# A decoder's third stage: squaring and applying a triangular matrix in one product, without GpSimd's additions

## The reference, cut to what matters

```
def step(S, t):                      # one token of a chunk, all heads
    k_t, v_t, a_t, b_t = t
    S = S * a_t[:, :, None]
    kTS = jnp.einsum('bd,bde->be', k_t, S)
    S = S + (b_t * k_t)[:, :, None] * (v_t - kTS)[:, None, :]
```

## Time and profile before

| | us |
|---|---|
| three runs | 2650.59, 2654.94, 2660.51 |
| median | 2654.94 |
| span of the profiled execution | 2659.3 |
| third stage in it | 933.5 to 2659.3 |
| busy in the span: PE, DVE, ACT, POOL | 2338.5, 1532.4, 1679.5, 295.0 |

### The profile page before, as it was taken

How to read it: one execution, slowest core, us unless ns; L and a number is a source line. 1 busy time by engine, 2 the same in 40 slices (tenths; PEclk the granted TensorE clock), 3 DMA queues, 4 the chain that set the end, 5 groups by cost and what they waited for, 6 DMA issues and landing times.

```text
span 2659.3 us, 93159 instructions
## 1 busy us (share of the span) xinstructions
PE 2338.5 (88%) x41310; PEld 1738.7 (65%) x41314; DVE 1532.4 (58%) x3564; ACT 1679.5 (63%) x4172; POOL 295.0 (11%) x396
## 2 busy tenths in 40 slices
PE   3888889888888479999989999999999999999997
PEld 2666666666666257767767667777676676676775
DVE  3565656656565546555555665556656656655563
ACT  2778778777877245655656656556656566565563
POOL 0101010110100000110011001101110110011010
PEclk8999999999999689999999999999999999999997
DMA  3000000000000100000000000000000000000000
GB/s 111 8 9 9 8 9 9 10 8 9 9 8 7 50 7 9 7 7 7 6 9 7 7 9 7 7 6 6 9 8 6 9 7 7 9 7 7 6 6 4
DMA packets 55339, 29.77 MB, mean 11 GB/s; under 512 B 24224, under 2 KB 53216, under 8 KB 54944
## 3 DMA queue, kind: packets, MB, share of 16 engines
q1 hardware_dynamic: 50624, 21.90, 3.0%
q10 hardware_dynamic: 4320, 1.97, 0.3%
HBM read 18.60 MB, written 5.24 MB: 9 GB/s over the span
## 4 chain that ended last, share of the span: by engine, by line
PE 38%; DVE 13%; ACT 11%; issue 2%; DMA 0%; SPq 0%; DVEq 0%
PE bank L1130 5%; PE bank L1197 2%; PE bank L1327 2%; ACT PT L1382 2%; DVE h L1530 2%; DVE zels L462 2%; PE bank L358 2%; PE bank L1260 2%; ACT zels L1382 2%; DVE m L458 2%; PE bank L1246 1%; DVE h L1643 1%; PE bank L1320 1%; PE bank L1170 1%; PE bank L1229 1%
## 5 line engine op out<-in xcount | busy, mean ns | idle before, releaser
L1040 POOL TENSOR_TENSOR PT<-zels,unit 128x512 f32<-128x512 f32 x160 | 203.7, 1273 | 1472.3 <-ACT zels L1382 1284.1
L358 PE MATMUL bank<-w_gate,ident 128*128 128x256 f32 (+3 forms) x960 | 314.5, 411 | 0.0
L458 DVE TENSOR_REDUCE m<-bank 128x4 f32<-128x512 f32 x384 | 251.6, 683 | 39.7 <-PE bank L383 19.2
L393 PE MATMUL bank<-ident,zels 128*128 128x128 f32 x1536 | 226.3, 282 | 34.3 <-ACT zels L429 26.9
L1382 ACT ACTIVATE zels<-bank 128x512 f32<-128x512 f32 (+1 forms) x256 | 142.6, 573 | 158.8 <-PE bank L1246 82.6
L393 PEld LDWEIGHTS bank<-ident,zels 128*128 128x128 f32 x1536 | 168.3, 142 | 83.4 <-ACT zels L429 38.4
L437 ACT ACTIVATE PT<-bank 128x512 f32<-128x512 f32 x384 | 206.1, 629 | 3.8 <-PE bank L393 2.9
L1382 ACT ACTIVATE PT<-bank 128x512 f32<-128x512 f32 x256 | 147.8, 598 | 89.7 <-PE bank L1303 47.7
L433 ACT ACTIVATE zels<-zels 128x512 f32<-128x512 f32 x256 | 162.7, 646 | 55.5 <-DVE zels L462 55.1
L429 ACT ACTIVATE zels<-bank,m 128x128 f32<-128x128 f32 x512 | 148.0, 389 | 64.7 <-DVE m L458 64.7
L462 DVE TENSOR_TENSOR zels<-bank,m 128x512 f32<-128x512 f32 x256 | 177.0, 692 | 8.9
(11 more groups left out here) (293 smaller groups left out, 5125.7 us busy)
## 6 DMA issues: line engine op xcount, KB each, us to landing
ctxT<-in_ctxT_dram SPq DMA_DIRECT2D x64, 48.0 KB, 1.8
x_after_cross_attention<-x SPq DMA_DIRECT2D x32, 64.0 KB, 1.5
h<-x_after_cross_attention SPq DMA_DIRECT2D x8, 256.0 KB, 2.8
xin<-x_after_cross_attention SPq DMA_DIRECT2D x32, 64.0 KB, 1.8
out_dram<-xn SPq DMA_DIRECT2D x32, 64.0 KB, 1.6
x<-in_xT_dram ACTq DMA_DIRECT2D x30, 64.0 KB, 1.8
input_integers<-xq SPq DMA_DIRECT2D x8, 128.0 KB, 2.0
xq<-input_integers SPq DMA_DIRECT2D x32, 32.0 KB, 1.8
```

The source lines that it names most:

```text
L358: mm(bank[:, 0:cols], ident[:, :], w_gate[:, :, :].rearrange("p a b -> p (a b)")[:, 0:cols], start=True, stop=True)
L393: last = xp(b[u][:, j * P:(j + 1) * P], n.zels[:, u, j * P:(j + 1) * P], ident[:, :])
L458: dve.tensor_reduce(top, scores, AX_X, ALU.max if t == "y" else ALU.min).then_inc(ph.dve[s], ph.DV.step(s, f"{t}max{u}"))
L1040: pool.tensor_tensor(n.TI[:, k % 2, :, :], (n.PT0, n.PT1)[k % 2][:, :, 1, :], unit[:, :].unsqueeze(1).broadcast_to([P, NP, DK]), ALU.add)\
```

## The change

T stays T on the left of its products: Bk squares the transpose (`T^T T^T`), and Lk multiplies from the right-hand side `[T | W]`, 128 columns wide, so that one product gives the square of T and T W. W is kept beside T in one buffer (`WTW`: W, T, W), on alternating sides. DVE adds T W to the old W (`grown`). POOL has no step in the third stage any more.

```diff
-            n.W = buf("W", [P, NP, DK])
+            n.eb = buf("eb", [P, NP, DK])
...
+            n.WTW = n.zels[:, 0:3, :].rearrange("p a b -> p (a b)").rearrange("p (h k t) -> p h k t", h=NP, k=3)
+            n.T, n.W = n.WTW[:, :, 1, :], [n.WTW[:, :, 2, :], n.WTW[:, :, 0, :]]
+            n.TT = [n.zels[:, 3, :].rearrange("p (h t) -> p h t", h=NP), n.eb[:, :, :]]
...
-        SOLVE = (*[x for k in range(LEVELS - 1) for x in (f"X{k}", f"W{k}")], "A", f"W{LEVELS - 1}")
+        SOLVE = (*[x for k in range(LEVELS - 1) for x in (f"B{k}", f"L{k}")], "A", "W")
...
-            "act": (35, "100010110100001101101011010011000101010100100110011101110110111001101100110110001101",
...
+            "act": (26, "101101001110101011000110100010100001011011001010010010001011100110011100011011110000",
...
-        def with_identity(pool, it, s, k):
...
-            pool.tensor_tensor(n.TI[:, k % 2, :, :], (n.PT0, n.PT1)[k % 2][:, :, 1, :], unit[:, :].unsqueeze(1).broadcast_to([P, NP, DK]), ALU.add)\
...
+                        if stage == f"B{k}":
+                            act_did("T0" if k == 0 else f"L{k - 1}0")
+                            held()
+                            for p, src, dst in tiles():
+                                last = mm(solve_out(p, dst, 2), n.T[src, p, :], TT[src, p, :], start=True, stop=True)
+                            last.then_inc(pc.pe[s], pc.PE.step(s, f"B{k}"))
...
+                        if stage == f"L{k}":
                             if k == 0:
+                                act_did("V")
+                                dve_did("cV1")
                             else:
+                                dve_did(f"L{k - 1}1")
                             held()
+                            for p, src, dst in tiles():
                                 if k < LEVELS - 2:
+                                    last = mm(n.psum[dst, p // 4, p % 4 * P:(p % 4 + 1) * P], TT[src, p, :], n.WTW[src, p, 1 - k % 2:3 - k % 2, :], start=True, stop=True)
+                                else:
+                                    last = mm(n.psum[dst, p // 4, p % 4 * P + DK:(p % 4 + 1) * P], TT[src, p, :], n.W[0][src, p, :], start=True, stop=True)
+                            if k == LEVELS - 2:
                                 for p, src, dst in tiles():
+                                    last = mm(n.psum[dst, p // 4, p % 4 * P:p % 4 * P + DK], n.Km[src, p, 0:DK], ident[src, src], start=True, stop=True)
+                            last.then_inc(pc.pe[s], pc.PE.step(s, f"L{k}"))
+                    if stage == "W":
+                        act_did(f"L{LEVELS - 2}0")
+                        dve_did(f"L{LEVELS - 2}1")
+                        held()
+                        for p, src, dst in tiles():
+                            last = mm(n.psum[dst, p // 4, p % 4 * P:p % 4 * P + DK], n.TT[(LEVELS - 1) % 2][src, p, :], n.W[1][src, p, :], start=True, stop=True)
+                        last.then_inc(pc.pe[s], pc.PE.step(s, "W"))
...
+                    elif stage == "V0":
+                        dve_did("cV0")
+                        f(n.W[0], n.cV[:, 0, :, :], ACT.Copy, "V")
...
+                    elif stage[0] == "B":
                         k = int(stage[1:])
...
+                        f(by_bank(n.TT[(k + 1) % 2]), solved(2), ACT.Copy, stage)
+                    elif stage[0] == "L":
...
+                        for i in (1, 0):
+                            if i == 0:
+                                dve_did(f"{stage}0")
+                            f((n.T if k < LEVELS - 2 else n.KmT)[:, 4 * i:4 * i + 4, :], pairs(i)[:, :, k % 2 * DK:(k % 2 + 1) * DK], ACT.Copy, f"{stage}{i}")
...
+                    def grown(k, i, name=None):
+                        at = slice((1 - k % 2) * DK, (2 - k % 2) * DK)
+                        was, now, more = n.W[k % 2][:, 4 * i:4 * i + 4, :], n.W[1 - k % 2][:, 4 * i:4 * i + 4, :], pairs(i)[:, :, at]
+                        if i == 0:
+                            last = dve.tensor_tensor(now, more, was, ALU.add)
+                        else:
+                            dve.tensor_tensor(now[0:DK], more[0:DK], was[DK:P], ALU.add)
+                            last = dve.tensor_tensor(now[DK:P], more[DK:P], was[0:DK], ALU.add)
+                        if name:
+                            then(last, name)
...
+                    elif stage[0] == "L":
...
+                        for i in range(2):
+                            if i == 1:
+                                act_did(f"{stage}1")
+                            grown(k, i, f"{stage}{i}")
+                    elif stage == "W":
+                        pe_did("W")
+                        grown(LEVELS - 1, 0)
+                        grown(LEVELS - 1, 1, "W")
```

More of the change, by code:

```diff
@@ L1035, in groups @@
             return [order[k:k + 4] for k in range(0, len(order), 4)]
-        def with_identity(pool, it, s, k):
-            n = lane[s]
-            pool.tensor_tensor(n.TI[:, k % 2, :, :], (n.PT0, n.PT1)[k % 2][:, :, 1, :], unit[:, :].unsqueeze(1).broadcast_to([P, NP, DK]), ALU.add)\
-                .then_inc(pc.pool[s], pc.PO.step(s, f"TI{k}"))
         def pe_norm(pe, it, s, t, stage):
@@ L1092, in _ @@
                     sp.wait_ge(pc.stored[s], 16 * ROUNDS + FIRST)
-            @block.gpsimd
-            def _(pool):
-                def advance(s, it, stage):
-                    n = lane[s]
-                    if stage == "T0":
-                        pool.wait_ge(pc.act[s], pc.AC.upto(it, "T0"))
-                        with_identity(pool, it, s, 0)
-                    for k in range(LEVELS - 2):
-                        if stage == f"X{k}":
-                            pool.wait_ge(pc.act[s], pc.AC.upto(it, f"X{k}"))
-                            pool.wait_ge(pc.dve[s], pc.DV.upto(it, f"X{k}"))
-                            if k > 0:
-                                pool.wait_ge(pc.pe[s], pc.PE.upto(it, f"W{k - 1}"))
-                            with_identity(pool, it, s, k + 1)
-                in_rounds(pool, advance, CSLOTS["pool"])
             @block.tensor
@@ L1228, in advance @@
                             for lo, hi in halves:
-                                last = mm(solve_out(p, slice(lo, hi), 2), n.PT0[lo:hi, p, 0, :], ident[lo:hi, lo:hi], start=True, stop=True)
+                                last = mm(solve_out(p, slice(lo, hi), 2), n.T[lo:hi, p, :], ident[lo:hi, lo:hi], start=True, stop=True)
                         last.then_inc(pc.pe[s], pc.PE.step(s, "T0"))
-                    for k in range(LEVELS):
-                        PT, W = (n.PT0, n.PT1)[k % 2], n.W if k > 0 else n.cV[:, 0, :, :]
-                        if stage == f"X{k}":
+                    for k in range(LEVELS - 1):
+                        TT = n.TT[k % 2]
+                        if stage == f"B{k}":
[5 more added lines that the diff above has]
+                        if stage == f"L{k}":
@@ L1235, in advance @@
                             if k == 0:
-                                act_did("T0")
-                            else:
-                                act_did(f"X{k - 1}")
-                                dve_did(f"X{k - 1}")
+                                act_did("V")
+                                dve_did("cV1")
+                            else:
+                                dve_did(f"L{k - 1}1")
                             held()
-                            for group in groups():
+                            for p, src, dst in tiles():
@@ L1242, in advance @@
                                 if k < LEVELS - 2:
-                                    for p, src, dst in group:
-                                        mm(solve_out(p, dst, 2, 0, P), PT[src, p, 1, :], PT[src, p, 0, :], start=True, stop=True)
-                                for p, src, dst in group:
-                                    last = mm(solve_out(p, dst, 2, DK, P), PT[src, p, 0, :], PT[src, p, 1, :], start=True, stop=True)
-                            last.then_inc(pc.pe[s], pc.PE.step(s, f"X{k}"))
@@ L1283, in advance @@
                     if stage == "S":
-                        act_did(f"W{LEVELS - 1}")
-                        dve_did("AT1")
+                        dve_did("W")
                         held()
                         for p, src, dst in tiles():
-                            last = mm(solve_out(p, dst, 2), n.KmT[src, p, :], n.W[src, p, :], start=True, stop=True)
+                            last = mm(solve_out(p, dst, 2), n.KmT[src, p, :], n.W[0][src, p, :], start=True, stop=True)
                         last.then_inc(pc.pe[s], pc.PE.step(s, "S"))
@@ L1597, in advance @@
                         dve_did("Mm")
[L1598 removed]
+                        then(dve.tensor_tensor(n.T, n.S[:, :, :], n.cds[:, 1, :].unsqueeze(2).broadcast_to([P, NP, DK]), ALU.mult), "P0")
                     elif stage == "V0":
@@ L1603, in advance @@
```

(8 more changed lines are left out.)

70 lines of the change are left out of this document (14 added, 56 removed).

## The result

| | before | after |
|---|---|---|
| median of the runs | 2657.7 (4 runs) | 2702.1 (4 runs, 2699.0 to 2708.8) |
| profiled execution, its span | 2659.3 | 2696.9 |
| products (records) of TensorE | 41310 | 36194 |
| instructions of VectorE / GpSimd | 3564 / 396 | 3980 / 236 |

The ratio is 1.0176, 95% interval 1.0154 to 1.0198. The forecast was 2650, the range 2612 to 2692: wrong in sign, and outside the range.

A forecast was written before the change was run, and what follows sets the result against it. TensorE was taken to bound the round, busy about 97 of 105.2 us. Work -23.7, fetching -6, waits +16.5 and ends +8 gave -5.2 on 2659.3: span 2654, median 2650; range 2612 to 2692.

The forecast's parts named there:

- the term of the new waits: TensorE's waits from the solve's longer chain and new order: 1.1 us a round net, 16.5 us over 15 rounds.
- 1.95 going: Old TensorE waits going or shrinking: attention's output 0.7, S before O 0.65, copy of X 0.4, spikes' norm 0.2 a round.
- The halving: Only half the net new waits counted, because one lane's wait lets the other chain run ahead: 1.1 us a round.
- The list: Places in the solve where TensorE waits bare, before B0 to B3 and S: 4.1 us a round.
- Their waits stay: Rest of the round keeps its phase with the lanes exchanged, so its waits were taken as unchanged.
- fetching: TensorE's waits called issue shrink with fewer products in the solve: 0.4 us a round, 6 us in all.
- both ends: Lane 1 starts later in the third stage, the last pass gives 3 to 6 us back: 8 us lost on the whole.
- the third rival: TensorE's clock falls once a round after longer waits in the solve, ten rounds more: +40 us, 2690; chance 0.08.
- The upper bound: Most that TensorE's new waits could cost, all counted in full: 4.1 us a round, 62 us.
- TensorE's work: Cheaper L0 to L3 and last W in the solve save 1.58 us a round, 23.7 us over 15 rounds.
- Rival 1: New TensorE waits replace later ones instead of adding; only work, fetching and ends count: 2633 us; chance 0.32.
- Rival 2: ScalarE and VectorE hold each other up at the solve's hand-overs: 2.8 us a round, 42 us, 2692; chance 0.19.

The follow-up runs named there:

- Run 12: Changed kernel, B1 to B4 multiplying the identity instead of the newest T, and VectorE's additions left out in levels 0 to 4: 2650.0 us.
- run 7: Changed kernel with one TensorE step moved: lane 1's third transposition of probabilities put ahead of lane 0's B2, covering a wait: 2707.6 us.
- run 5: Changed kernel without VectorE's additions on the first four pairs in levels 0 to 4, so ScalarE copies its second half without waiting: 2697.9 us.
- run 6: Changed kernel without VectorE's two additions on the second four pairs in levels 0 to 4, hand-over to B unchanged: 2694.6 us.
- run 2: Changed kernel's new solve put in the step order of the kernel before, two steps moved: 2932.1 us.
- run 10: Changed kernel, B1 to B4 multiplying the identity instead of the newest T, so B no longer waits for L's copies: 2679.8 us.
- run 9: Kernel before, with a sixth identity addition on GpSimd so that the last W has 16 products instead of 32: 2639.3 us.
- run 1: Old solve of the kernel before, put in the changed kernel's step order: 2731.1 us.
- run 4: Kernel before with another order of the same steps on all four engines: 2666.7 us.
- run 11: Kernel before with a sixth GpSimd addition, last W of 16 products, and steps reordered on all four engines: 2632.1 us.

## Why the prediction was wrong

- **The step that failed** is the term of the new waits: 4.1 of bare places less 1.95 going, of which "I count half of the difference, rounded up: 1.1 a round". Measured are +4.0. The 2.9 between them have three parts of like size. The halving is 1.05 (2.15 less 1.1): its reason, that a lane's wait lets the other chain run ahead so that later waits shrink, gave no net gain. The list was 0.9 short: 5.0 measured, with B0 and S longer and one place missing. And outside the solve 5.1 a round are left, not the 6.1 - 1.95 = 4.15 of the forecast, again 0.9. "Their waits stay" was wrong there in both directions: 3.0 went where 1.95 were listed, and 2.0 came where none were. The halving alone is 16 us, and the forecast without it would have been 2666, still too fast.
- **In the sum of the span** the miss is 42.8 us (37.6 + 5.2): waits 43.5 too few over 15 rounds, work and fetching 7.2 better than forecast, both ends equal, 6.5 ahead of the stage. Run 12 shows the waits from the other side: 2.3 a round of the solve's are away, about 34 us over 15 rounds, and 50 us are back, the rest from fewer pauses called issue and less busy time.
- **What was overlooked in the rows:** the longest wait before was 1.1 us and not 0.9 (L372, which the earlier trace rows leaves out), and it was the one that shrank most. The clock was below 1.00 in three rounds before the change; the third rival counted one.
- **The upper bound** was the second failure: 62 us stood in the text as a bound of this term, and the sum with it would have been 2695. The range ended at 2692, since no rival had the waits simply in full. The measured 4.0 a round lies just within the bound.
- **TensorE's work** was right in kind and too small: L at 1.02 as taken, but the busy time fell by 2.6 a round and not by 1.58. B ahead of an L costs 0.49 and not 0.62, which no term had. The rows called issue fell by 0.1, where I had put 0.4.
- **The ends** came out: +13.2 and -5.3, 7.9, forecast 8.
- **Rival 1** (waits move) is true in part of one wait (run 7) and false of all (run 12). **Rival 2** came nearest in time with a wrong mechanism: its levels stayed covered, the waits in the solve's lines are 5.0 a round and not above 6, and runs 5 and 6 take away its cause without its price. **Rival 3**, the clock, is below 1.00 in 5 rounds instead of 3, about 0.1 us a round; run 2 shows what it would have taken.
- **Not foreseen:** 6.5 us ahead of the third stage. GpSimd's first operation of the first stage starts late. Before, then after:

```profile
43.99 0.40 POOL L691 TENSOR_TENSOR ls<-x 128x128 f32<-128x128 f32 x1 [41.74 <-DMA x<-in_xT_dram]
```
```profile
49.55 0.76 POOL L691 TENSOR_TENSOR ls<-x 128x128 f32<-128x128 f32 x2 [47.31 <-issue]
```

It waits for nothing that the profile shows. The third stage begins at 937.4 to 938.0 in all five kernels with GpSimd's additions, and at 942.2 to 944.7 in all nine without them. These nine also share the new solve, so that it comes with GpSimd's program in the third stage is likely and not shown, nor is the path.

## What to carry to other kernels

Before a chain gets a longer hand-over to save products, write down what stands bare at each level, and count those waits in full; only a run that covers them may discount them. With a new order, list the waits outside the chain again as well: here 3.0 a round went and 2.0 came. A hand-over made shorter can only gain up to the next one behind it (runs 5 and 10). Work taken off TensorE where no wait comes with it is time saved one for one (run 9). An order of steps belongs to its chain: compare two chains each in an order of its own.

## What the runs showed of the hardware

- **VectorE beside GpSimd.** Two operations of VectorE from SBUF to SBUF with one tensor input took 1.49 us (L1534, run 1) and 1.38 us (L1536, run 4) instead of 0.42 when they started while an addition of GpSimd ran; one of the convolution with two tensor inputs took 1.37 instead of 0.34 (L1522, runs 9 and 11). Each ended 0.15 to 0.29 us after that addition. L1534 kept its 0.41 where the addition began after it (run 4). Operations that read PSUM kept their time (copies of X, L1610, 0.69). "GPSIMD Engine Reference" of the Trainium skill, section "1. Specifications", says that GpSimd's SBUF interfaces are shared with VectorE, and that they contend with VectorE's instructions in a 2-port mode or with two SBUF inputs. The convolution's row agrees; in which mode the other two ran, no trace shows. The price was the rest of the running addition.
- **TensorE's pauses have fixed places.** I counted TensorE's records from the start of the span, weight loads, products and semaphore instructions together. Pauses of over 0.55 us inside a block, where products of one line follow each other and that line does not always pause, are 25 from 1000 to 2540 us before the change, and each begins at record 246 or 247 modulo 256. After the change there are 15, all at 250 or 251, and in run 1 there are 33, all at 246 or 247. A pause does not come at every such place. "Advanced Engine Details and Errata" of the Trainium skill, section "ISA Cache", gives 256 instructions to a line of 16 KB, which agrees with the spacing. That a refill is late there would fit, but no run here changed it.
